# Attention and two 1-bit convolutions: the negated row maxima in fp16, turned into rows by fp16 products with an fp16 identity

## What is computed

```python
xn = group_norm(x)
q, k, v = split(qkv_weight @ xn + qkv_bias)          # 4 heads of 64, 4096 positions
attn = softmax(q k / sqrt(64))
x = x + proj_weight @ (attn v) + proj_bias
out = relu(batch_norm(x)); out = conv3x3(out, mean|w0| * sign(w0))
out = relu(batch_norm(out)); out = conv3x3(out, mean|w1| * sign(w1))
return out + x
```

## Time and profile before

| | |
|---|---|
| median of 3 runs | 2878.78 us (2878.61 to 2879.64) |
| the profiled execution's own time | 2875.61 us |
| its span, first to last instruction | 2873.6 us |
| mean granted TensorE clock | 0.993 of full speed |
| PE busy | 2773.8 us, 97% |
| VectorE busy | 2106.7 us, 73% |
| GpSimd busy | 2014.4 us, 70% |
| ScalarE busy | 1415.1 us, 49% |

### The profile page before, as it was taken

The page is one execution under the profiler, slowest core; times in us unless marked ns, Lnnn a source line. Parts: engine busy times, 40 slices in busy tenths (PEclk is TensorE's granted clock), DMA queues, the critical chain, the costliest instruction groups (busy, mean ns, idle before and its releaser), DMA issues. The chain is left out here.

```text
span 2873.6 us, 43432 instructions
## 1 busy us (share of the span) xinstructions
PE 2773.8 (97%) x17060; PEld 1011.4 (35%) x17060; DVE 2106.7 (73%) x2496; ACT 1415.1 (49%) x1493; POOL 2014.4 (70%) x1192
## 2 busy tenths in 40 slices
PE   5999999999999999999999999989999999899898
PEld 2333333334333333334333333343333333344343
DVE  5788888727788888457888888277778885598785
ACT  3455555554555555544555555545555555254342
POOL 2688888894888888855888888948888888400022
PEclk9999999999999999999999999999999999999999
DMA  5100000001000000041000000000000000421022
GB/s 218 50 1 1 1 1 1 1 1 65 1 1 1 1 1 1 1 148 50 1 1 1 1 1 1 1 30 1 1 1 1 1 1 1 151 81 61 20 97 88
DMA packets 26818, 78.26 MB, mean 27 GB/s; under 512 B 1920, under 2 KB 2176, under 8 KB 25600
## 3 DMA queue, kind: packets, MB, share of 16 engines
q1 hardware_dynamic: 25648, 73.01, 7.2%
q10 hardware_dynamic: 976, 2.63, 0.3%
HBM read 58.86 MB, written 16.78 MB: 26 GB/s over the span
## 5 line engine op out<-in xcount | busy, mean ns | idle before, releaser
L540 POOL TENSOR_TENSOR acc_pool<-acc_pool,prob 128x512 f32<-128x512 f32 (+1 forms) x992 | 1780.6, 1795 | 294.8 <-ACT prob L609 173.6
L609 ACT ACTIVATE prob<-ps,exp_scale 128x1024 f32<-128x1024 f32 x1024 | 1088.0, 1110 | 980.2 <-PE ps L776 974.0
L867 DVE TENSOR_REDUCE m_part<-ps 128x2 f32<-128x1024 f32 x1024 | 1246.3, 1222 | 433.7 <-PE ps L730 409.8
L760 PE MATMUL ps<-prob,vals 128*64 128x512 f32 x4096 | 991.1, 605 | 0.0
L760 PEld LDWEIGHTS ps<-prob,vals 128*64 128x64 f32 x4096 | 248.8, 136 | 501.7 <-issue 363.8
L730 PE MATMUL ps<-k_hi,q_hi 64*128 64x512 f16 x2048 | 391.1, 383 | 15.9 <-DVE m_part L867 9.6
L776 PE MATMUL ps<-m_rows,shift 64*128 64x512 f16 x2048 | 389.1, 376 | 2.9 <-DVE m_rows L894 2.9
L771 PE MATMUL ps<-q_hi,k_hi 64*128 64x512 f16 x2048 | 389.9, 377 | 0.0
L771 PE MATMUL ps<-q_lo,k_hi 64*128 64x512 f16 x2048 | 389.0, 376 | 0.0
L771 PE MATMUL ps<-q_hi,k_lo 64*128 64x512 f16 x2048 | 389.0, 376 | 0.0
L936 DVE TENSOR_TENSOR ps<-ps,prob 128x512 f32<-128x512 f32 x480 | 331.5, 691 | 72.4 <-ACT prob L609 72.4
(11 more groups left out here) (112 smaller groups left out, 1455.4 us busy)
## 6 DMA issues: line engine op xcount, KB each, us to landing
xt<-in_x SPq DMA_DIRECT2D x32, 512.0 KB, 4.4
xf<-in_x SPq DMA_DIRECT2D x4, 2048.0 KB, 16.5
xn<-in_x SPq DMA_DIRECT2D x16, 512.0 KB, 7.1
x_scratch<-y_tile SPq DMA_DIRECT2D x16, 512.0 KB, 5.2
rows<-x_scratch SPq DMA_DIRECT2D x8, 576.0 KB, 5.1
rows<-x_scratch SPq DMA_DIRECT2D x8, 544.0 KB, 4.6
xt<-x_scratch SPq DMA_DIRECT2D x4, 1024.0 KB, 5.2
y_tile<-x_scratch SPq DMA_DIRECT2D x4, 1024.0 KB, 5.1
```

The costliest lines, as they stand in the source:

```text
L540: nc.gpsimd.tensor_tensor(acc[:, part], acc[:, part], tile[:, part], ALU.add).then_inc(pool_add, 1)
L609: nc.scalar.activation(prob[:, n % PBUF], g.ps_s[:, kt % 2].rearrange("p h n -> p (h n)"), ACT.Exp, scale=g.exp_scale[:]).then_inc(exp_don ...
L760: last = mm(g.ps_o[own[h], :], vals[:, kt, own[h]], prob[:, n % PBUF, h * TB:(h + 1) * TB], start=(kt == 0), stop=(kt == KT - 1))
L867: v.tensor_reduce(m_part[:, block % 2, :, u], source, AX.X, ALU.max).then_inc(mx_used, 1)
```

## The change

`m_neg` becomes an fp16 tensor, which VectorE writes directly. A new fp16 tensor `ident16` is filled once by ScalarE with a copy of the fp32 identity, as ScalarE's first instruction in `attention`. The two products of `max_rows` take both operands in fp16. TensorE waits for the new semaphore `ident_ready` ahead of each of them.

```diff
-        m_neg = sb("m_neg", [P, 2 * QT])
+        m_neg = sb("m_neg", [P, 2 * QT], F16)
+        ident16 = sb("ident16", [P, P], F16)
...
+        ident_ready = sem("ident_ready")
...
             act.sem_inc(o_copied, 1)
+            nc.scalar.activation(ident16[:], ident, ACT.Copy).then_inc(ident_ready, 1)
 
             for s in range(2):
                 for c in range(CB):
...
             def max_rows(it):
+                pe.wait_ge(ident_ready, 1)
                 pe.wait_ge(m_neg_ready, it + 1)
                 for h in range(2):
-                    last = mm(g.ps_misc[0:QT, h * P:(h + 1) * P], m_neg[:, h * QT:(h + 1) * QT], ident,
+                    last = mm(g.ps_misc[0:QT, h * P:(h + 1) * P], m_neg[:, h * QT:(h + 1) * QT], ident16[:],
                               start=True, stop=True)
                 last.then_inc(m_rows_ready, 1)
```

## The result

| | before | after |
|---|---|---|
| median of 13 runs each | 2878.95 us (2876.25 to 2884.36) | 2870.92 us (2869.38 to 2876.12) |
| ratio, 95% interval | | 0.9974 (0.9965 to 0.9982) |
| the profiled execution's time | 2875.61 us | 2870.17 us |
| its span | 2873.6 us | 2868.2 us |

The change makes the kernel faster by 0.26%, between 5 and 10 us; the medians lie 8.0 us apart. The head of the page after answers to the earlier trace rows: PE has 64 records fewer (its products are as many as before), ScalarE has one instruction more, the copy, and the other engines' work is what it was.

What follows compares the result with a forecast made beforehand. The prediction took PE's queue to pace the query blocks: 8.1 us saved in blocks plus 1.2 at pair starts, less 0.3 for the copy, took the median from 2878.8 to 2869.8 us. The range was 2866.0 to 2873.5 us.

Steps and rivals of the forecast that it cites:

- PE's queue sets the pace of a block: In query blocks, time taken out of PE's queue comes off the end: 0.31 us in each of 26 blocks, 8.1 us.
- The turn of form: Into and out of the `max_rows` products, changing product form costs 0.09 us each way; both turns stay.
- The distance of two short products: In `max_rows`, the second fp16 product starts 0.06 us after the first; with the skill's 81 ns the gain is smaller.
- Rival 1: In `max_rows`, a short product costs its 0.109 us slot, not its columns: 0.22 us less per occurrence, 2872.5 us; chance 0.14.
- The cap by VectorE: Behind `max_rows` in a block, VectorE's next reduction lets at most 0.44 us of PE's saving through.
- Pair starts: At the four pair starts PE is a link in the chain with VectorE: 0.31 us less each, 1.2 us together.
- two occurrences caught by GpSimd: At the end of each batch's first pair, PE waits for GpSimd's total: no gain, wait grows from 0.58 to about 0.9 us.
- The once-a-block wait: Around group 7 of each block PE waits for VectorE, 9.6 us in total; it moves with PE and takes nothing.
- rival 2: The once-a-block wait for VectorE takes the blocks' gain, growing to nearly 18 us; only 0.9 us gained, 2877.9 us; chance 0.08.
- The copy: At the start of `attention`, ScalarE's added copy is on the path and costs 0.3 us once, bounds 0 and 0.63.
- The sum: Over the whole kernel, 9.3 us gained less 0.3 us added makes 9.0 us less: 2869.8 us.
- Rival 4: At block turns or pair starts the clock falls, about 1.4 us lost each; at all 32 occurrences 2914.6 us; chance 0.03.

Runs made afterwards that it cites:

- e8: The kernel before, products still fp32, with `m_neg` padded by zeros to 64 columns for each head; 2875.65 us in a single run.
- e7: The changed kernel with `m_neg` padded by zeros to 64 columns for each head; 2869.13 us in a single run.
- e12: The changed kernel with the two fp16 products of `max_rows` done twice over, into the same places; 2875.52 us in a single run.
- e1: The kernel before with only the fp16 identity copy and the wait for it added, products still fp32; 2879.01 us, ratio 1.0003.
- e2: The changed kernel with the `max_rows` products at the four pair starts fp32 again; 2873.12 us, ratio 0.9982 to the kernel before.
- e6: The kernel before run again, nothing changed; 2876.30 us.
- e3: The changed kernel run again, nothing further changed; 2872.81 us, ratio 0.9982 to the kernel before.
- e11: The kernel of e5 with `m_neg` padded to 64 columns for each head; 2861.72 us, ratio 0.9945.
- e4: The changed kernel with twelve score products of the first two key tiles put ahead of `max_rows` at the pair starts; 2869.39 us, ratio 0.9965.
- e9: The kernel before, fp32 products and no copy, with e5's rearrangement filling PE's pauses at the pair starts; 2875.52 us, ratio 0.9988.
- e5: The kernel of e4 with the second key tile's products moved behind `max_rows` and extra score products filling both pair-start pauses; 2864.49 us, ratio 0.9956.
- e10: The kernel of e5 run again, nothing further changed; 2864.09 us.

## Why the prediction was right

- **PE's queue sets the pace of a block, and 0.31 us less in it come off.** Right: 0.33 us less from L730 to L760, 0.33 less for each block. The terms by themselves: 0.31 to the first product (0.31 said, and shown to be the form's, since the types are now alike), 0.05 to 0.057 to the second (0.06), 0.15 to L760 (0.15).
- **The turn of form costs 0.09 us without a change of type.** Right, and shown in e8 for the way out of `max_rows`: at fp32 it fell from 0.20 to 0.11 us when the form stayed. The 0.10 us that e8's blocks won are in part overlap. The Trainium skill's rule in TensorEngine Tiling (Array Packing), section Key Properties, that a change of tiling mode drains TensorE, agrees in kind; the size here is 0.1 us.
- **The distance of two short products.** The figure of the Trainium skill that the prediction set beside its own, 81 ns for such pairs (TensorE: Matmul & The Clock Gate, section Back-to-back issue gap), is not what this kernel shows: 0.055 us with weights of 4 columns, for two or four such products in a row. With weights of 64 columns, in e7, the two stand 0.08 us apart (166.47 and 166.55). Rival 1, a slot of 0.109 us, is refuted by e12, where the same products with weights of 4 columns stand 0.057 us apart.
- **The cap by VectorE** was worked out as 0.44 us and measured as 0.39 (e7). It didn't bind at 0.33 except for 0.01 us. The bound took the reduction to start when `m_rows` is written, at 0.20 us before its present start; the 0.05 us that it missed are of the size of one hand-over: in e7 `m_rows` is written at 167.72 + 1.38 = 169.10 and the reduction starts at 169.14.
- **Pair starts** 0.33 (0.31 said); **two occurrences caught by GpSimd**: right, the wait went from 0.58 to 0.95 us (about 0.9 said), and the two turns of pairs gained nothing; those without a fall are 128.4 to 128.6 us long in kernels of either kind.
- **The once-a-block wait** stayed at 9.6 us, so rival 2 is refuted at the place where it had to show itself.
- **The copy** costs 0.22 us, for 0.3 said. Its length was right (0.31 us), but ScalarE starts the next instruction before it ends. The sign given for it, a first L691 at 38.1 us, did not come, because it was a time from the start of the execution and that start varies by more.
- **The sum** should then be 9.6 us; the medians differ by 8.0 (5 to 10 by the interval), and the profiled executions by 5.4. The forecast of 9.0 had no term for what the stretches outside the blocks do from one execution to the next: falls of the clock behind PE's pauses, and stores that land late. That 9.0 lies so near to 8.0 is in part luck: the gain was put 0.6 us too low and these losses at nothing.
- **Rival 4, the clock,** was right about the mechanism and named the right places, the pair starts. Its price of 1.4 us is near most of the falls found (0.9 to 1.3 us; a few cost up to 3.9). A fall does not need the shorter work: e1, e2 and e6 have them with fp32 products at the starts. The argument against it, a clock of 1.00 over 100 to 1240 us, was no evidence: the mean of so long a stretch rounds a fall away, that very trace has one at 650.3 us, and e6 shows that the next execution has them at the pair starts too.

Left open: whether the change lowers the clock by a little after all. The mean granted clocks of the runs say that it may: 0.9907 over the nine runs of e3 and 0.9908 over the eleven of e2, against 0.9917 over the 26 runs of the kernel before taken beside them (standard errors of 0.0002 to 0.0003). A thousandth of 2875 us is an estimated 3 us of TensorE's work, and what is missing between 9.6 us and the differences of the medians (8.0, and 5.7 in e3) is of that size. The traces can't say where: 9 of 16 pair starts with fp16 products against 9 of 20 with fp32 ones is no difference, and at the two turns of pairs there is a fall in 15 of 18 cases in kernels with fp16 blocks and in 5 of 10 in those with fp32 blocks, which can still be chance. The longer wait for GpSimd ahead of a turn does not decide by itself: the kernel before fell behind a wait of 0.58 us, and e11 did not behind one of 1.08. No run here changed only that wait.

## What to carry to other kernels

Where one engine is busy without a pause, the cost of an instruction is the distance between starts around it, and it can be taken apart into columns, turns of form and hand-overs; each of the parts taken so was right here to a few hundredths of a microsecond. A small gain has to be looked for stretch by stretch, since executions of one and the same kernel differ by almost as much as it brings (2875.5 to 2884.4 us for the kernel before). A mean clock of 1.00 over a long stretch hides short falls, so ask for the clock just behind each pause. Pauses of TensorE of one to two microseconds are worth filling with work that is at hand, even with products that nobody needs: at these pair starts they cost nothing, as the stretches are the 64.0 us of e4's one start without a fall, and the clock held in 16 of 16 cases, in four traced executions. They are no warrant for a whole run, as the seven longer runs of e9 show, and the pauses of 2.86 us at the turns of pairs were left as they are.

## What was not expected of the hardware

- The clock falls by chance behind the same pauses: in 21 of 40 unfilled pair starts, with 1.87 us idle, 1.0 us of work (1.4 with fp32 products) and 0.73 us idle there (or 1.49 us idle behind the work, e4). It costs 0.9 to 3.9 us each time, and nothing at all in other executions of the same kernel.
- Products of the form 128*64 overlap where they write different halves of the output's partitions: in e7 the first value product starts 0.01 us after the first product of `max_rows`, whose columns alone take 0.05 us.
- By the medians the gain of the filled kernels looks larger than their falls at the pair starts explain: e5 lies 6 to 8 us under the changed kernel's two medians. In the profiled executions nothing is left over. e3's is 8.3 us longer than e5's: 6.0 in the first stretches (2.6 for the score products ahead, 3.4 for three falls), 0.9 ahead of the first `max_rows`, where e3's clock is at 0.50 from 48.5 to 51.9 us and e5's is not, 0.3 at the turn of batches and 1.1 behind the last `max_rows`. Why the runs of e5, e10 and e11 spread so little was not followed up.
